# A three-layer graph network on one core: node rows moved as 112 and 13 partitions, gather lists kept on chip, another order of stores at the end of layer 0

## What is computed

```
def conv(h, W, b):
    m = jnp.concatenate([h[dst], h[src], edge_attr], axis=1) @ W + b
    return jax.ops.segment_sum(m, dst, num_segments=n_nodes)
h = jax.nn.relu(conv(x, W1, b1))
h = jax.nn.relu(conv(h, W2, b2))
return conv(h, W3, b3)
```

## Time and profile before

| | |
|---|---|
| median of three runs | 3284.95 us |
| the profiled execution | 3291.26 us |
| its span, first to last instruction | 3289.5 us |
| TensorE busy | 2855.1 us (87%) |
| GpSimd busy | 2341.1 us (71%) |
| DVE busy | 1466.7 us (45%) |
| ScalarE busy | 1247.5 us (38%) |
| mean granted TensorE clock | 0.963 of full |
| moved | 508.17 MB, mean 154 GB/s |
| ScalarE's and SP's queues, packets | 111192 and 183583 |

### The profile page before, as it was taken

How to read it: one execution, slowest core, us unless ns; L and a number is a source line. 1 busy time by engine, 2 the same in 40 slices (tenths; PEclk the granted TensorE clock), 3 DMA queues, 4 the chain that set the end, 5 groups by cost and what they waited for, 6 DMA issues and landing times.

```text
span 3289.5 us, 62730 instructions
## 1 busy us (share of the span) xinstructions
PE 2855.1 (87%) x22952; PEld 1708.8 (52%) x22952; DVE 1466.7 (45%) x3427; ACT 1247.5 (38%) x2139; POOL 2341.1 (71%) x2868
## 2 busy tenths in 40 slices
PE   0059999999999999999828999999998899987988
PEld 0025555655555555555515665566665555544645
DVE  5468888888888888888100101001111111111111
ACT  1058888888888888888000000000000000000000
POOL 2717888888888888888347877677747766655653
PEclk9989999999999999999968999999998999988989
DMA  2135354444445444444856999899987989977972
GB/s 53 33 72 151 108 153 125 137 142 118 138 124 152 107 127 131 123 136 123 207 124 161 217 214 215 190 214 218 215 201 174 205 184 202 207 173 166 205 167 67
DMA packets 338277, 508.17 MB, mean 154 GB/s; under 512 B 253775, under 2 KB 289750, under 8 KB 309850
## 3 DMA queue, kind: packets, MB, share of 16 engines
q1 hardware_dynamic: 183583, 289.68, 36.2%
q10 hardware_dynamic: 111192, 151.49, 17.3%
q0 software_dynamic: 43200, 62.97, 9.5%
HBM read 352.40 MB, written 151.51 MB: 153 GB/s over the span
## 4 chain that ended last, share of the span: by engine, by line
PE 54%; POOL 18%; DMA 8%; DVE 7%; ACTq 6%; issue 5%; ACT 2%; SPq 0%; POOLq 0%; DVEq 0%
PE ps L1096 26%; PE ps L1104 14%; POOL far_rows L675 7%; PE ps L1077 6%; DMA dst_stage<-in_dst 4%; ACTq L480 3%; PE ps L1157 2%; ACTq L514 2%; POOL blocks L662 2%; PE ps L1158 2%; POOL attr_stage L704 2%; DVE is_key L913 2%; ACT blocks L781 1%; POOL attr_parts L709 1%; DMA far_rows<-parts,far_src 1%
## 5 line engine op out<-in xcount | busy, mean ns | idle before, releaser
L675 POOL DMA_INDIRECT far_rows<-parts,far_src x1200 | 1292.0, 1077 | 574.9 <-issue 297.9
L1096 PE MATMUL ps<-blocks,parts 125*128 125x400 fp8e4 x7500 | 1669.5, 337 | 3.5 <-ACT blocks L781 1.8
L781 ACT ACTIVATE blocks<-ps 125x505 fp8e4<-125x505 f32 x2000 | 1164.0, 731 | 187.1 <-PE ps L1077 179.8
L1096 PEld LDWEIGHTS ps<-blocks,parts 125*128 125x128 bf16 x7500 | 750.0, 101 | 456.0 <-issue 29.2
L1077 PE MATMUL ps<-is_key,is_low 128*125 128x505 bf16 x2000 | 767.3, 391 | 62.2 <-DVE is_key L913 54.8
L1104 PE MATMUL ps<-blocks,parts 125*64 125x400 fp8e4 x7500 | 723.9, 337 | 0.0
L913 DVE TENSOR_SCALAR is_key<-from_one,parts 128x500 bf16<-128x500 f16 x2000 | 682.8, 390 | 34.1 <-PE ps L1077 29.7
L977 DVE COPY z<-ps 125x256 f32<-125x256 f32 x75 | 31.9, 425 | 1426.9 <-PE ps L1158 1426.9
L1104 PEld LDWEIGHTS ps<-blocks,parts 125*64 125x64 bf16 x7500 | 387.5, 110 | 320.5 <-issue 161.3
L1077 PEld LDWEIGHTS ps<-is_key,is_low 128*125 128x125 bf16 x2000 | 274.3, 138 | 321.2 <-DVE is_key L913 142.6
L806 ACT COPY acc_sb<-ps 128x500 f32<-128x500 f32 x50 | 28.8, 576 | 929.0 <-PE ps L1132 684.3
(11 more groups left out here) (101 smaller groups left out, 1473.1 us busy)
## 6 DMA issues: line engine op xcount, KB each, us to landing
blocks<-counts SPq DMA_DIRECT2D x100, 1137.5 KB
counts<-blocks ACTq DMA_DIRECT2D x25, 4375.0 KB
blocks<-counts SPq DMA_DIRECT2D x100, 1050.0 KB
far_rows<-parts,far_src POOLq DMA_INDIRECT x1200
attr_stage<-in_edge_attr SPq DMA_DIRECT2D x250, 64.0 KB
blocks<-counts SPq DMA_DIRECT2D x100, 132.0 KB
counts<-blocks ACTq DMA_DIRECT2D x25, 507.8 KB
blocks<-counts SPq DMA_DIRECT2D x100, 121.9 KB
```

The costliest lines, as they stand in the source:

```text
L675: nc.gpsimd.indirect_dma_start(far_rows[:, g % 2, h, j, :], None, parts_d[layer], bass.IndirectOffsetOnAxis(ap=far_src[:, g % LISTED, h, j ...
L781: nc.scalar.activation(blocks[0:L, b % 2, :, n * W:(n + 1) * W], build[0:L, c % BUILD, 0:COLS].rearrange("p (t w) -> p t w", w=W), ACT.Cop ...
L1096: nc.tensor.matmul(acc_ps(g), parts[0:L, layer % 2, t, 0:2, :].rearrange("p k d -> p (k d)"), blocks[0:L, g % 2, t, :], start=(t == 0), st ...
```

## The change

- `load_h`, `load_x` and `store_nodes` move 125 rows in two transfers, of 112 and 13 rows (`ROWS`), and the waits count two.
- Between layers h lies in `rows_d`, ordered by batch and partition, so that a partition's four rows of 64 features are one piece of 1 KB. x and the output keep pieces of 256 B.
- `far_src` and `far_dst` hold the lists of all 25 batches. The target lists of the last two groups of a batch are loaded by `load_group` straight to `far_dst`, the source lists by `load_far` on SP in layer 0; in layers 1 and 2 nothing is loaded for them.
- At the end of layer 0 ScalarE issues the store of the attribute sums of batch 24 first, then its parts and rows, then the loads of h and of the sums for batch 26; SP no longer issues the store, nor the h load of batch 26, and its load of the sums for batch 25 stands ahead of the block loads for batch 26.

```
@@ tensors
-    far_src = sb("far_src", [P, LISTED, FAR, J], i32)
-    far_dst = sb("far_dst", [P, LISTED, FAR, J], i32)
+    far_src = sb("far_src", [P, BATCHES, FAR, J], i32)
+    far_dst = sb("far_dst", [P, BATCHES, FAR, J], i32)
+    rows_d = [nc.dram_tensor(f"rows_{n}", (BATCHES, L, T, D), fp32).ap() for n in range(1, LAYERS)]
@@ load_h
-            engine.dma_start(h_rows[:, g % 2, :, :],
-                         feats[layer][b * B:(b + 1) * B, :].rearrange("(t p) d -> p t d", p=L)
-                         ).then_inc(h_loaded[g % 2], DMA)
+            table = rows_d[layer - 1][b, :, :, :] if layer else x[b * B:(b + 1) * B, :].rearrange("(t p) d -> p t d", p=L)
+            for r in range(2):
+                rows = slice(ROWS[r], ROWS[r + 1])
+                engine.dma_start(h_rows[rows, g % 2, :, :], table[rows, :, :]).then_inc(h_loaded[g % 2], DMA)
@@ load_x
-            engine.dma_start(x_rows[:, g % 2, :, :], x[b * B:(b + 1) * B, :].rearrange("(t p) d -> p t d", p=L)
-                         ).then_inc(x_loaded[g % 2], DMA)
+            table = x[b * B:(b + 1) * B, :].rearrange("(t p) d -> p t d", p=L)
+            for r in range(2):
+                rows = slice(ROWS[r], ROWS[r + 1])
+                engine.dma_start(x_rows[rows, g % 2, :, :], table[rows, :, :]).then_inc(x_loaded[g % 2], DMA)
@@ store_nodes
-            engine.dma_start(table[b * B:(b + 1) * B, :].rearrange("(t p) d -> p t d", p=L),
-                         node_rows[:, g % 2, :, :]).then_inc(nodes_stored[g % 2], DMA)
+            for r in range(2):
+                rows = slice(ROWS[r], ROWS[r + 1])
+                engine.dma_start(table[rows, :, :], node_rows[rows, g % 2, :, :]).then_inc(nodes_stored[g % 2], DMA)
@@ load_group
-                sp.dma_start(dst_stage[:, s, :], dst[bass.ds(start, GROUP)].rearrange("(p j) -> p j", j=J)
+                into = dst_stage[:, s, :] if h < 0 else far_dst[:, b, h, :]
+                sp.dma_start(into, dst[bass.ds(start, GROUP)].rearrange("(p j) -> p j", j=J)
@@ SP, end of layer 0
             load_h(sp, BATCHES)
-            for q in range(4):
-                load_block(BATCHES + 1, q)
-            store_attr(BATCHES - 1)
             load_attr(sp, BATCHES)
-            load_h(sp, BATCHES + 1)
-            for g in range(BATCHES + 2, ALL):
+            for g in range(BATCHES + 1, ALL):
                 for q in range(4):
                     load_block(g, q)
@@ ScalarE, end of layer 0 and layers 1 and 2
-            load_attr(act, BATCHES + 1)
-            load_far(act, BATCHES + 1)
-            load_far(act, BATCHES + 2)
+            store_attr(act, BATCHES - 1)
             store_parts(act, BATCHES - 1)
             store_nodes(act, BATCHES - 1)
+            load_h(act, BATCHES + 1)
+            load_attr(act, BATCHES + 1)
...
-                if g + 3 < ALL:
-                    load_far(act, g + 3)
```

More of the change, by code:

```diff
@@ L45, in gnn_kernel @@
     WORDS = TILES * DENSE // 2
-    LISTED = 4
     PAUSES = [0, 5, 10]
@@ L215, in gnn_kernel @@
         w_loaded = sem("w_loaded")
-        far_src_loaded = [sem(f"far_src_loaded{k}") for k in range(LISTED)]
-        far_dst_loaded = [sem(f"far_dst_loaded{k}") for k in range(LISTED)]
+        far_src_loaded = [sem(f"far_src_loaded{k}") for k in range(2)]
         far_landed = [sem(f"far_landed{k}") for k in range(2)]
@@ L502, in start_of @@
             return engine.value_load(group_start[0:1, n:n + 1], min_val=0, max_val=E - GROUP)
[L504 to L518, removed]
         def far_group(g, h):
@@ L585, in load_group, with load_far @@
                              ).then_inc(attr_landed[s], DMA)
-                sp.dma_start(dst_stage[:, s, :], dst[bass.ds(start, GROUP)].rearrange("(p j) -> p j", j=J)
+                b, k = divmod(n, PER_BATCH)
+                h = k - (PER_BATCH - FAR)
+                into = dst_stage[:, s, :] if h < 0 else far_dst[:, b, h, :]
+                sp.dma_start(into, dst[bass.ds(start, GROUP)].rearrange("(p j) -> p j", j=J)
                              ).then_inc(attr_landed[s], DMA)
-            def store_attr(b):
-                sp.wait_ge(attr_kept, b + 1)
-                sp.dma_start(attr_sums[b, :, :], own_sb[D:OWN, b % 2, :]).then_inc(attr_stored[b % 2], DMA)
+            def load_far(b):
+                for h in range(FAR):
+                    start = start_of(sp, b * PER_BATCH + PER_BATCH - FAR + h)
+                    sp.dma_start(far_src[:, b, h, :], src[bass.ds(start, GROUP)].rearrange("(p j) -> p j", j=J)
+                                 ).then_inc(far_src_loaded[b % 2], DMA)
             sp.wait_ge(x_split, 1)
@@ L612, in _ @@
                         if k == 1:
-                            store_attr(g - 1)
+                            store_attr(sp, g - 1)
                         elif k == 2 and g + 1 < BATCHES:
                             load_h(sp, g + 1)
-                        elif k == 3:
-                            load_far(sp, g + 1)
-                if g == BATCHES - 1:
-                    for q in range(4):
-                        load_block(BATCHES, q)
+                        elif k == 3 and g + 1 < BATCHES:
+                            load_far(g + 1)
+                    if k == PER_BATCH - RING and g == BATCHES - 1:
+                        for q in range(4):
+                            load_block(BATCHES, q)
                 if g >= 1:
@@ L668, in gather_rows @@
                 if h == 0 and j == 0:
-                    pool.wait_ge(far_src_loaded[g % LISTED], (g // LISTED + 1) * FAR * DMA)
+                    if layer == 0:
+                        pool.wait_ge(far_src_loaded[g % 2], (g // 2 + 1) * FAR * DMA)
                     if g % BATCHES <= 1:
@@ L714, in make_rows @@
                 if g >= 2:
-                    pool.wait_ge(nodes_stored[g % 2], g // 2 * DMA)
+                    pool.wait_ge(nodes_stored[g % 2], g // 2 * 2 * DMA)
                 for t in range(T):
@@ L723, in scale_rows @@
             def scale_rows(b):
-                pool.wait_ge(h_loaded[b % 2], (b // 2 + 1) * DMA)
+                pool.wait_ge(h_loaded[b % 2], (b // 2 + 1) * 2 * DMA)
                 if b == 0:
@@ L1136, in turn_h @@
             def turn_h(g):
-                pe.wait_ge(h_loaded[g % 2], (g // 2 + 1) * DMA)
+                pe.wait_ge(h_loaded[g % 2], (g // 2 + 1) * 2 * DMA)
                 if g < BATCHES:
```

28 lines of the change are left out of this document (17 added, 11 removed).

## The result

| | before | after |
|---|---|---|
| median, runs | 3285.42 us, 4 (3276.99 to 3302.06) | 3201.95 us, 4 (3199.22 to 3205.65) |
| ratio, 95% interval | | 0.9741 (0.9701 to 0.978) |
| profiled execution, span | 3291.26, 3289.5 | 3200.72, 3198.8 |

Faster by 83 us in the medians and by 90.5 in the profiled executions. The forecast was 161 (3124, range 3092 to 3192): nearly twice what came, and 3202 lies above the range.

What follows compares the result with a forecast made beforehand. TensorE was taken as the bound in layer 1 (29.64 us a batch), with pauses elsewhere; 89 + 49.5 + 19 + 3.5 = 161 us off 3291.3 gave 3130, by the median 3124 us, range 3092 to 3192.

Steps and rivals of the forecast that it cites:

- Part 1: Layers 1 and 2: split rows and no list loads end ScalarE's held issues, `own_sb` waits and slow restarts; 89 us.
- 3284.95, 6.3 lower: Last step: median of the runs shown against the profiled execution's 3291.3, taking the forecast from 3130 to 3124 us.
- Part 2: End of layer 0: ScalarE stores sums and parts first, so GpSimd's first gather starts earlier; 49.5 us.
- the 2.9: End of layer 0: gain from having no four list issues between ScalarE's two copies; 2.9 us.
- 0.36 us each: End of layer 0: time per piece taken for the parts store's 32 pieces, giving 11.5 us and landing at 1629.
- Rival 1: End of layer 0: the parts store still needs 31.2 us beside block loads; 19.5 us less gained, 3143; chance 0.15.
- 46.6: End of layer 0: how much earlier, in us, GpSimd's first gather starts once the parts land at 1629.
- Part 3: Layer 0: fewer pieces ahead of target lists shorten DVE's waits in long batches; 19 us (15 plus 4).
- the list is in SP's queue behind the 100-piece row store: Layer 0: reason given for late target lists in five long batches; the change takes 68 pieces off that spot.
- The lower bound that I named: Layer 0, five long batches: 0 us gained if the counts store alone sets the list's landing; upper bound 25.
- Part 4: Parts landing earlier between layers 1 and 2 (2 us) and last output store ending earlier (1.5); 3.5 us.
- Rivals 2 and 3: First: split doesn't shorten ScalarE's issues, 3190, chance 0.15; second: layer 2 bound by transfer engines, slower, 3339, chance 0.08.

Runs made afterwards that it cites:

- e12: The kernel before, unchanged, profiled on chip 13 in the same call as the changed kernel; median 3269.2 us.
- e13: The changed kernel, unchanged, profiled on chip 13 in the same call as the kernel before; median 3170.3 us.
- e5: The kernel before, unchanged, profiled once more, on chip 4; 3301.3 us (one run).
- e7: The kernel before with only the new order of ScalarE's stores and loads at the end of layer 0, on chip 4; median 3255.1 us.
- e2: The kernel before with only its two list tiles enlarged (25 slots instead of 4, 4 still used), on chip 11; median 3276.5 us.
- e8: The changed kernel with all rows moved whole again (125 rows, 256 B pieces), lists on chip and new order kept, on chip 4; median 3231.6 us.
- e6: The changed kernel with the two 25-slot list tiles allocated last, so other tiles keep their addresses of before, on chip 4; median 3197.0 us.

## Why the prediction was wrong, by its steps

**Part 1 (89 us).** The mechanism was right in each reading: issues of 125-row transfers held, `own_sb` late, slow restarts. Against the first trace the size was right too: layers 1 and 2 shrank by 86, in e12 and e13 by 96 (the forecast for this stretch, with what parts 2 and 4 add to it, was 94). What failed is the step from one trace to the median, "3284.95, 6.3 lower". It assumed that the trace's parts are as usual when its total is. They were not: layers 1 and 2 were at the long end (1524.5; the other traces with whole rows and list loads have 1523.6, 1504.5, 1495.5 and 1473.4, so their median, 1504.5, is 20 lower), layer 0 at the short end of what the chips show, and the two hid each other. The kernel before scatters over 3230 to 3305 us on chip 13 (e12's profile is its longest run), the changed one over 3162 to 3174, and TensorE's waits for `own_sb` are 84.6, 84.6, 63.6, 60.5 and 24.6 us over the whole of the five traces named (before, e12, e5, e7, e2). So what is held differs from run to run, and the split takes the scatter away too. In medians part 1 is worth an estimated 98 - 33 - 2 = 63 us on chip 13 and 81 - 28 = 53 on chip 11 (from the table; the intervals of the two differences are some 25 and 7 us to either side). On chip 14 it was measured nearly by itself: e9, the split alone, gives 87 (15 to either side), 2 to 5 of it in the hand-over (144.3 against 146.2 to 149.3). So 89 was clearly too much on chip 11 and need not have been on chip 14.

**Part 2 (49.5 us).** The order did what was said and nothing new blocks; the conv after the second copy came 3.1 us sooner, as the 2.9 said. The term that was mis-sized is "0.36 us each", 11.5 us for the parts: it was 26.7 to the first gather, 0.8 us each. I took the mean over a queue of small pieces in a stretch where block rows were not always beside them: from 1638.8 to 1675.5 the transfers had a share of 0.90 and 199 GB/s (0.27 and 69 from 1670 to 1680), from 1645 to 1672 in the changed kernel 1.02 and 252. Rival 1 (31.2 us, priced at 3143) was nearer, and its sign, 25 us or more, showed. For the first gather 46.6 became 32.6, for the whole hand-over 32.3. But it was wrong to leave that as fixed: with SP's loads held the store takes 3 to 10 us.

**Part 3 (19 us).** Nothing that can be told from chance: 2 us on chip 13, 1.7 on chip 4. The step that failed is "the list is in SP's queue behind the 100-piece row store": with those pieces gone the list is late all the same. The lower bound that I named, 0 if the counts store alone sets it, was nearest; that the counts store sets it is what is left, not shown.

**Part 4 (3.5 us)** is below what can be told apart; the time after the last copy fell by 0.6.

**Rivals 2 and 3.** e8 against e6 on one chip (3231.6 and 3197.0 us) and e9 refute 2. 3 did not show: in layer 2, where it was priced, TensorE is busy in all 400 us of 2700 to 3100, with the transfer engines' share at 0.94.

So of the 78 us that were missing in the medians, about 17 are part 3, 14 to 17 part 2, and 36 on chip 11 (26 on chip 13) what part 1 fell short of its 89; these shares are estimates, each with the scatter of the kernel before in it, and the rest is below what the comparisons can tell. In the two first traces 70.5 us were missing: 47.4 in layer 0, of which 28.4 are the difference between the groups of chips, 14.3 in the hand-over, 8 in layers 1 and 2.

## What to carry to other kernels

Cut the trace of before into stages and ask how much each scatters before subtracting terms from it: a total near the median says nothing of its parts. If a stage holds random stalls, its trace is one draw. Before a change is blamed or praised for a stage it hardly touches, profile both kernels on one chip, one right after the other. And a small store that something waits for should not run beside a queue of large rows: holding back block loads for some 10 us, where nobody needed them yet, gave 16 us and more.

## What was not expected of the hardware

Five chips (or the five times at which they were used) fall into two groups for the same program: layer 0 in 1596 to 1619 or 1625 to 1638 us. The price of a piece of a store goes from at most 0.1 us (3.0 us for 32) to 0.8 us by what another engine's queue holds. And one more issue of ScalarE shows how long a queue can hold one: in e8, where the hand-over was no longer for it (116.0 us, e6 on the same chip 115.1):

```profile
1638.23 37.12 ACTq L465 DMA_DIRECT2D h_rows<-feats  x1
```
